# The experts' second bias: from a product ahead of each second layer to a loaded row that VectorE adds

## Chip, cores and metric

One core of one Trainium2 chip runs the whole kernel as one program. The metric is the device time of one execution in microseconds (us). Engine names as the profile has them: PE is TensorE, DVE is VectorE, ACT is ScalarE, POOL is GpSimd, SP is SyncE; L1279 is line 1279 of the kernel before.

## The reference, cut to what matters

A graph layer and a linear-attention layer are added onto 12,500 nodes of 256 values; then comes a layer of 8 experts of which each node uses one. The change is in the last lines: what an expert adds as `b2`.

```python
xn = layernorm(x)
x = x + gnn(xn, src, dst, edge_weight, ...) + mix(xn, ...)      # 212,500 edges
h = layernorm(x)
idx = argmax(softmax(h @ gate_w + gate_b))                      # 8 experts
prb = the probability of idx
pos = how many nodes before this one chose the same expert
kept = pos < C                                                  # C = ceil(1.25 * 12500 / 8) = 1954
buf[idx, pos] = h                                               # for the kept ones
hmid = relu(buf @ w1[e] + b1[e])                                # 256 -> 1024
ybuf = hmid @ w2[e] + b2[e]                                     # 1024 -> 256
y = ybuf[idx, min(pos, C - 1)] * (prb * kept)[:, None]
x = x + nan_to_num(y, posinf=10000, neginf=-10000)
```

## The kernel before, in words

The five engines run five programs that meet in semaphores; each engine's order is written out ahead of time. The order goes by *places*, 266 of them. At each of the first 208 (`PAIRS`) POOL gathers 8 chunks of 128 node rows for the edges (`gather_rows`, L967, one indirect DMA per chunk, two halves with the other POOL work of the place between them) and PE multiplies the place's 8 chunks into windows of sums (`multiply_pair`, L1079; the row buffers hold 6 places). What else is done at a place stands in the list `side`: "kv" (the attention's sums), "early" and "late" (the node tiles, `c_step`), "unit" (the experts), "end" (routing after place 208). A planner puts the experts' ticks there by estimated PE costs (`PE_PLACE`, `PE_EXPERT`, `PE_TURN`) and due times (`wanted_at`); the change leaves it as it is.

**Routing.** The node tiles are routed in 18 batches. When a batch's experts are chosen (`choose_expert`), its tokens ranked (`place_tokens`) and full tiles of 128 tokens of one expert found (`find_full`, `queue_units`), `fill_slots` writes for each tile which rows to gather (`gat_i`), where to scatter (`sca_i`), the probabilities (`sprb`) and the expert (`expert_i`), and raises `q_ready`. The last batch has what is left over: 22 tiles. In all there are 105 tiles (`SLOTS`) in K = 82 units: units 0 to 22 have two tiles, 23 to 81 one. Units 60 to 81 are the last batch.

**A unit's way.** POOL gathers its tokens' rows, 256 normalised values and 256 to add to (`gather_unit`, L987). PE transposes the first (L1238), ACT copies them (L2042). Then come ticks, 4 in a unit of two tiles and 2 in a unit of one: PE's first layer (L1261), ACT's relu with `b1` (L2059), and one tick later PE's second layer (`second_layer`, L1285), summed in one PSUM bank. After the last, ACT scales the sum by the probability into `tok` (L2065), and VectorE's `finish_unit` makes not-a-number to 0 and clips (L1816 to L1820), adds the row's old value (L1821) and raises `y_done`. Up to place 207 SP keeps the finished rows in DRAM (`keep_unit`, units 0 to 52, 76 tiles); POOL scatters them to the output after place 208, two or four tiles at a place, from a row buffer that SP reloads (`load_back`, L841, 8 tiles at a time, waiting for the scatters of the buffer's tiles before; `scatter_back`, L1008). Units 53 to 81 are scattered straight from `tok` (`scatter_unit`, L998).

**Weights.** 1 MB each for first and second layer, two buffers each. Up to unit 63 SP loads them: `load_first` (L815) when unit k-2's relu is done, `load_second` (L822) when its second layer is; each reads the expert's number first. SP's queue is in order. For units 64 to 81 (`SKIPS`) POOL issues them as indirect loads (`load_new_first` L1017, `load_new_second` L1025), where the rows of an expert that the buffer holds already are left out. In the last batch POOL has at each unit: L1017, L987, two L1008, L998, L1025.

**The second bias before.** At the laps step SP loads `ffn_b2` twice; `make_tables` splits it in a high and a low part (`b2_parts`, 16 rows: 2 x 8 experts); `fill_slots` makes for each tile a column with 1 in its expert's two rows (`expert_hot`, L1713). At a unit's first tick VectorE's `unit_tick` waits until PE has done the first tick of the previous unit's second layer and spreads that column over 128 columns (`hot_wide`, L1803, semaphore `hot_spread`). PE's `second_layer` begins, for each tile, with the product of `hot_wide` and `b2_parts` (L1279, 16x128 by 16x256 in f32r), onto which the layer's 8 products of 128x128 by 128x256 are summed.

## Time and profile before

| | |
|---|---|
| median of 3 runs | 2501.23 us (2500.39 to 2503.88) |
| the profiled execution | 2497.35 us, of which span 2495.6 us |
| granted TensorE clock, mean | 0.93 |
| busy: PE, DVE, ACT, POOL | 82%, 61%, 41%, 74% |
| DMA | 568.84 MB, mean 228 GB/s |
| SP's loads by size | weights 64 + 64 of 1,028 and 1,024 KB; most others 128 KB |

A row of the profile's groups reads: line, engine, operation, what it writes <- what it reads, shape, count | busy us in total, mean ns of one | idle us of the engine just before them, with what ended that idle time. A row of the timeline reads: start us, duration us, engine, line, operation [idle before <- releaser]. SPq is SP's DMA queue. A row by windows reads: stretch, its length, then busy us (and instructions) of PE, PE's weight loads, DVE, ACT, POOL, then the granted clock, the share of DMA busy, and GB/s. PE runs each f32 product as two instructions. A wait for several semaphores is put down to the one that came last by the profile, and "issue" is time in which an engine waited for nothing that the profile shows.

### The profile page before, as it was taken

Reading aid. Unit: us, or ns where it says so; the run is one execution under the profiler, and the core shown is the slowest. Engines: PE = TensorE matmul, PEld = TensorE weight load, DVE = VectorE, ACT = ScalarE, POOL = GpSimd, SP = SyncE. Lnnn points to the kernel's source line nnn. Section 1 sums busy time; section 2 is a strip of 40 time slices with the busy share of each in tenths; the row PEclk is TensorE's granted clock in tenths of the full one; section 3 lists DMA queues with packets and bytes.
Section 4 is the critical chain, followed back from the end, with each engine's and each line's share of the span. In section 5 each row is a group of like instructions: output and inputs, shape, how many; then the busy total and the mean of one; then the engine's idle time right before and its main releaser. Section 6 shows DMA issues by size and latency. Waiting matters only on the chain. (4 is left out here: it accounts for less than half of the span.)

```text
span 2495.6 us, 42607 instructions
## 1 busy us (share of the span) xinstructions
PE 2049.6 (82%) x12873; PEld 1578.1 (63%) x12873; DVE 1511.6 (61%) x5293; ACT 1033.6 (41%) x2479; POOL 1849.9 (74%) x1924
## 2 busy tenths in 40 slices
PE   0048999994677787998989989998989998787997
PEld 0015666662455565776768777776778777676986
DVE  6776555554358777787747556566565666565332
ACT  4663333331244444543434433443444444352332
POOL 7777777777777777777777777777777777765575
PEclk9999999996788887999999999999998999898999
DMA  9846666664566667777777777777887888778653
GB/s 337 321 138 178 174 175 175 175 172 128 150 195 201 194 190 255 237 238 222 244 232 227 248 231 234 233 229 253 304 295 273 306 304 293 249 274 305 239 180 108
DMA packets 279195, 568.84 MB, mean 228 GB/s; under 512 B 51493, under 2 KB 180142, under 8 KB 259791
## 3 DMA queue, kind: packets, MB, share of 16 engines
q0 software_dynamic: 98352, 268.90, 35.3%
q1 hardware_dynamic: 150225, 245.97, 28.9%
q10 hardware_dynamic: 30390, 51.21, 5.6%
q8 instruction: 108, 1.77, 0.3%
q14 instruction: 120, 0.98, 0.1%
HBM read 506.09 MB, written 87.86 MB: 238 GB/s over the span
## 5 line engine op out<-in xcount | busy, mean ns | idle before, releaser
L967 POOL DMA_INDIRECT rows_sb<-xn_scratch,src_sb x1517 | 1458.3, 961 | 462.2 <-issue 456.7
L1261 PE MATMUL bank<-acc 128*128 128x128 f32 (+1 forms) x2624 | 434.4, 319 | 3.6 <-ACT acc L2042 2.9
L1285 PE MATMUL bank<-acc 128*128 128x256 f32 x1680 | 413.1, 390 | 0.0
L1261 PEld LDWEIGHTS bank<-acc 128*128 128x128 f32 x2624 | 379.2, 202 | 27.3 <-issue 5.6
L1079 PE MATMUL bank<-rows_sb,s_sb 128*24 128x256 f32 x3082 | 229.7, 419 | 198.6 <-DMA rows_sb<-xn_scratch,src_sb 198.0
L2059 ACT ACTIVATE acc<-bank,acc 128x128 f32<-128x128 f32 (+1 forms) x656 | 211.9, 398 | 368.5 <-PE bank L1261 368.2
L1285 PEld LDWEIGHTS bank<-acc 128*128 128x128 f32 x1680 | 313.9, 194 | 48.8 <-issue 0.4
L1549 DVE TENSOR_TENSOR acc<-acc,bank 128x48 f32 x831 | 170.5, 205 | 264.8 <-PE bank L1089 150.2
L1079 PEld LDWEIGHTS bank<-rows_sb,s_sb 128*24 128x24 f32 x3082 | 85.5, 108 | 272.8 <-issue 240.4
L1976 ACT COPY sums<-bank 120x256 f32<-120x256 f32 x208 | 76.5, 368 | 355.6 <-PE bank L1079 355.5
L2007 ACT ACT_TABLE_LOAD x95 | 121.9, 1283 | 200.8 <-PE bank L1168 199.9
L1109 PE MATMUL bank<-arena 128*128 128x512 f32 x392 | 184.1, 592 | 0.0
L1153 PE MATMUL bank<-arena,weff 128*128 128x128 f32 (+1 forms) x784 | 124.3, 310 | 35.4 <-ACT arena L2031 35.4
L1153 PEld LDWEIGHTS bank<-arena,weff 128*128 128x128 f32 x784 | 114.9, 218 | 51.1 <-issue 48.3
L1625 DVE TENSOR_TENSOR arena<-bank,bias_sb 128x256 f32<-128x256 f32 x98 | 41.3, 422 | 171.9 <-PE bank L1168 171.7
L987 POOL DMA_INDIRECT acc<-h_scratch,gat_i x105 | 101.5, 966 | 37.5 <-issue 31.1
L1816 DVE TENSOR_TENSOR acc<-acc 128x256 int32<-128x256 f32 x105 | 45.0, 428 | 132.2 <-ACT acc L2065 126.5
L1164 PE MATMUL bank<-w2m_sb,arena 128*128 128x256 f32 x392 | 118.6, 432 | 2.6 <-DVE arena L1630 2.6
L1991 ACT ACTIVATE arena<-bank 128x512 f32<-128x512 f32 x98 | 58.5, 597 | 143.0 <-PE bank L1100 141.7
L1166 PE MATMUL bank<-w1g_sb,arena 128*128 128x256 f32 x392 | 112.5, 414 | 0.0
L1089 PE MATMUL bank<-ident,sums 120*128 120x120 f32 x416 | 81.3, 278 | 33.6 <-DVE acc L1549 33.4
L1563 DVE TENSOR_TENSOR arena<-bank,ss 128x512 f32<-128x512 f32 x98 | 67.8, 691 | 64.0 <-PE bank L1100 61.4
(277 smaller groups left out, 3633.7 us busy)
## 6 DMA issues: line engine op xcount, KB each, us to landing
acc<-ffn_first_in SPq DMA_DIRECT2D x64, 1028.0 KB
acc<-ffn_w_in SPq DMA_DIRECT2D x64, 1024.0 KB
arena<-xn_scratch SPq DMA_DIRECT2D x194, 128.0 KB, 3.1
h_scratch<-arena ACTq DMA_DIRECT2D x97, 256.0 KB
rows_sb<-xn_scratch,src_sb POOLq DMA_INDIRECT x1517
xnt_scratch<-arena SPq DMA_DIRECT2D x97, 128.0 KB, 2.3
arena<-xnt_scratch SPq DMA_DIRECT2D x97, 128.0 KB
arena<-x_in SPq DMA_DIRECT2D x97, 128.0 KB
```

What stands on the lines that cost most here:

```text
L967: pool.indirect_dma_start(out=chunk_row(c), out_offset=None, in_=xn_d, in_offset=bass.IndirectOffsetOnAxis(ap=src_sb[:, c:c + 1], axis=0)) ...
L987: pool.indirect_dma_start(out=tok[:, col % TOKENS, :], out_offset=None, in_=h2_d[0:tokens, :], in_offset=bass.IndirectOffsetOnAxis(ap=gat_ ...
L1079: m = pe.matmul(psum[0][i * COLS:i * COLS + WIN, 0:D], s_sb[:, p % S_SLOTS, i * GROUP + j, :], chunk_row(c), start=j == 0, stop=j == GROUP ...
L1109: m = pe.matmul(kv[0:r, :], xnt[:, t % R1, h, 0:r], wkv_sb[:, h, :], start=False, stop=h == H - 1)
L1153: m = pe.matmul(psum[2][:, f * P:f * P + r], weff[:, h, f * P:(f + 1) * P], c_xnt[:, t % XS, h, 0:r], start=h == 0, stop=h == H - 1)
L1164: pe.matmul(mix, c_hid[:, par, f, 0:r], w2m_sb[:, f, :], start=f == 0, stop=f == H - 1)
L1166: pe.matmul(gnn, c_xnt[:, t % XS, h, 0:r], w1g_sb[:, h, :], start=h == 0, stop=False)
L1261: m = pe.matmul(bank[:, i * tokens:(i + 1) * tokens], w1_sb[k % 2][:, h, f * P:(f + 1) * P], xt[:, k % 2, h, 0:tokens], start=h == 0, stop ...
L1285: m = pe.matmul(bank[:, i * D:(i + 1) * D], hid[:, f, i * P:(i + 1) * P], w2_sb[k % 2][:, f, :], start=False, stop=f == FC - 1 and i == 0)
L1549: dve.tensor_tensor(win, win, turned[:, :, i * COLS:i * COLS + WIN], ALU.add).then_inc(grp_added, 1)
L2007: act.activation(c_hid[:, par, f, 0:r], psum[2][:, f * P:f * P + r], ACT.Gelu, bias=beff[:, f:f + 1]).then_inc(c_gelu, 1)
L2059: act.activation(hid[:, f, 0:tokens], bank[:, i * tokens:(i + 1) * tokens], ACT.Relu, bias=b1_sb[k % 2][:, f:f + 1]).then_inc(l1_relu, 1)
```

## The change

The bias product, its split table, the one-hot columns and the copy that spread them are taken out. Instead there are two buffers of 128x256, `b2_sb`. SP loads for each unit the row `ffn_b2[expert]` into all 128 partitions (`load_bias`), at the place after the one where unit k-2 is finished, behind all else that SP has at that place, and waits for `y_done` of unit k-2. `finish_unit` waits for that load and begins for each tile with one operation more: y = bias x probability + y, ahead of the clean-up. The second layer's first product now starts the sum. The counts that `w2_ld` is waited for change as the two early loads go.

```diff
@@ -277,14 +277,12 @@
         w1_sb = [v[:, 0:H * FF].rearrange("p (h f) -> p h f", h=H) for v in first_sb]
         b1_sb = [v[:, H * FF:] for v in first_sb]
         w2_sb = [behind(0, FC, D) for _ in range(2)]
-        b2_parts, hot_wide = bkv_hl[0:2 * NE, 0:D], ones_r[0:2 * NE, :]
-        expert_hot = behind(1, SLOTS)[0:2 * NE, :]
+        b2_sb = [behind(1, D) for _ in range(2)]
         tok = behind(1, TOKENS, 2 * D)
         xt = behind(1, 2, H, UNIT)
         hid = behind(1, FC, UNIT)
         mask_sb = behind(1, D)
         clip_sb = behind(1, D)
-        b2_raw, b2_high = clip_sb[0:2 * NE, :], mask_sb[0:2 * NE, :]
 
         tab = behind(1, 2 * P)
         e_wide = behind(0, P)
@@ -294,8 +292,8 @@
         sel = behind(1, 2 * MOST_SLOTS)
         load_row = behind(1, MOST_SLOTS).bitcast(I32)
         sprb = behind(0, SLOTS)
-        (col_i, col_odd, col_tile, col_from, full_at, one_at, some_at, count, full, fresh, ranked, queue_at, queue_base, expert_no) = (
-            behind(0, 1) for _ in range(14))
+        (col_i, col_odd, col_tile, col_from, full_at, one_at, some_at, count, full, fresh, ranked, queue_at, queue_base) = (
+            behind(0, 1) for _ in range(13))
 
 
         ld_gmin, ld_edges, gmin_all = sem("ld_gmin"), sem("ld_edges"), sem("gmin_all")
@@ -307,7 +305,7 @@
             sem("early_stats"), sem("early_root"), sem("early_scaled"), sem("early_normed"))
         xn_ld, xnt_st = sems("xn_ld", R1), sems("xnt_st", R1)
         c_ld, cr_ld, c_st = sems("c_ld", XS), sems("cr_ld", RS), sems("c_st", OS)
-        w1_ld, w2_ld = sems("w1_ld", 2), sems("w2_ld", 2)
+        w1_ld, w2_ld, b2_ld = sems("w1_ld", 2), sems("w2_ld", 2), sems("b2_ld", 2)
         xs_ld, y_st = sems("xs_ld", 4), sems("y_st", YS)
         assert BACK_SLOTS * BACK_ROWS <= ROW_SLOTS
         kept_st, back_ld, back_st = sems("kept_st", YS), sems("back_ld", BACK_SLOTS), sems("back_st", BACK_SLOTS)
@@ -338,7 +336,7 @@
         q_fresh, q_selected, q_ready = sem("q_fresh"), sem("q_selected"), sem("q_ready")
         x_turned, x_copied = sem("x_turned"), sem("x_copied")
         l1_mm, l1_relu, l2_mm = sem("l1_mm"), sem("l1_relu"), sem("l2_mm")
-        y_scaled, y_done, hot_spread = sem("y_scaled"), sem("y_done"), sem("hot_spread")
+        y_scaled, y_done = sem("y_scaled"), sem("y_done")
 
 
         def halves(w):
@@ -607,11 +605,12 @@
             return e_place[last_tick[k] + FLUSH]
 
 
-        w1_at, w2_at, gather_at, scatter_at = ([[] for _ in range(PLACES)] for _ in range(4))
+        w1_at, w2_at, b2_at, gather_at, scatter_at = ([[] for _ in range(PLACES)] for _ in range(5))
         for k in range(K):
             known = slots_at[batch_of[k]] + 1
             w1_at[max([known] + [place_of(k - 1, 1)] * (k > 1))].append(k)
             w2_at[max([known] + [place_of(k - 1, 2)] * (k > 1))].append(k)
+            b2_at[max([known] + [done_place(k - 2) + 1] * (k > 1))].append(k)
             lag = wanted_at[k] - slots_at[batch_of[k]] - 1
             ahead = 1 if turn_place[k] < PAIRS + 2 else 3
             asked = max(known - 1 + lag, turn_place[k] - ahead)
@@ -652,7 +651,7 @@
             return 16 * ((k - SKIPS[0]) // 2 + 1)
 
         def w2_value(k):
-            return 16 * (k // 2 + 1) + 32 * (k % 2 == 0)
+            return 16 * (k // 2 + 1)
 
         def kv_steps(k, order):
             return [(k - s, s) for s in order if 0 <= k - s < T]
@@ -821,6 +820,13 @@
                     sp.wait_ge(l2_mm, l1_done(k - 2))
                 sp.dma_start(flat2(w2_sb[k % 2]), ffn_w2[bass.ds(x_, 1)].rearrange("a p f -> p (a f)")
                              ).then_inc(w2_ld[k % 2], 16)
+
+            def load_bias(k):
+                x_ = expert_of(k)
+                if k >= 2:
+                    sp.wait_ge(y_done, k - 1)
+                sp.dma_start(b2_sb[k % 2], ffn_b2[bass.ds(x_, 1), :].broadcast_to([P, D])
+                             ).then_inc(b2_ld[k % 2], 16)
 
             def keep_unit(k):
                 col, n = columns_of(k)[0], size(k)
@@ -859,8 +865,6 @@
                         for to, frm in ((w2m_sb[:, :, :], halves(mix_w2)), (w1g_sb[:, :, :], halves(gnn_w1t)),
                                         (w2g_sb[:, :, :], halves(gnn_w2t))):
                             sp.dma_start(to, frm).then_inc(wld2, 16)
-                        for part in range(2):
-                            sp.dma_start(b2_raw[part * NE:(part + 1) * NE, :], ffn_b2).then_inc(w2_ld[0], 16)
                     elif kind == "early":
                         for t, s in c_steps(k, (2, 0, 3)):
                             if s == 0:
@@ -879,6 +883,8 @@
                         load_second(k)
                 for k in keep_at[p]:
                     keep_unit(k)
+                for k in b2_at[p]:
+                    load_bias(k)
             for t in range(max(0, T - OS), T):
                 sp.wait_ge(c_st[t % OS], 32 * (t // OS + 1))
 
@@ -1272,18 +1278,13 @@
                         pe.wait_ge(new2_ld[k % 2], new_value(k))
                     else:
                         pe.wait_ge(w2_ld[k % 2], w2_value(k))
-                    pe.wait_ge(hot_spread, k + 1)
                     if y_bank_before(k) is not None:
                         pe.wait_ge(y_scaled, columns_of(y_bank_before(k))[-1] + 1)
-                    for i, col in enumerate(columns_of(k)):
-                        pe.matmul(bank[:, i * D:(i + 1) * D], hot_wide.bitcast(F32R), b2_parts.bitcast(F32R),
-                                  start=i == 0, stop=False)
-
                 for f in range(per_tick(k) * (j - 1), per_tick(k) * j):
                     tiles = range(size(k))
                     for i in tiles if f < FC - 1 else reversed(tiles):
                         m = pe.matmul(bank[:, i * D:(i + 1) * D], hid[:, f, i * P:(i + 1) * P], w2_sb[k % 2][:, f, :],
-                                      start=False, stop=f == FC - 1 and i == 0)
+                                      start=f == 0 and i == 0, stop=f == FC - 1 and i == 0)
                 m.then_inc(l2_mm, 1)
 
             def side_step(kind, k):
@@ -1668,14 +1669,6 @@
                 link(dve.tensor_scalar(some_at, col_tile, float(P), 1.0, ALU.mult, ALU.add))
                 for v in (tab, full, queue_at, queue_base):
                     link(dve.memset(v, 0.0))
-                link(dve.tensor_single_scalar(expert_no, ids[:, 0:1], 1.0, ALU.subtract))
-                link(dve.tensor_copy(whole, expert_no))
-                link(dve.tensor_single_scalar(whole, whole, NE - 1, ALU.bitwise_and))
-                link(dve.tensor_copy(expert_no, whole))
-                dve.wait_ge(w2_ld[0], 32)
-                link(dve.tensor_copy(b2_high.bitcast(F32R), b2_raw))
-                link(dve.tensor_tensor(b2_parts.bitcast(F32R), b2_raw, b2_high, ALU.subtract))
-                link(dve.tensor_copy(b2_parts[0:NE, :].bitcast(F32R), b2_high[0:NE, :]))
 
 
             def find_full(b):
@@ -1710,8 +1703,6 @@
                 token, chance, expert = (psum[6][:, SLOT_AT + i * n:SLOT_AT + (i + 1) * n] for i in range(3))
                 idf, empty = sel[:, 0:n], sel[:, MOST_SLOTS:MOST_SLOTS + n]
                 link(dve.tensor_copy(expert_i[:, here], expert[0:1, :]))
-                link(dve.tensor_scalar(expert_hot[:, here], expert[0:2 * NE, :], expert_no[0:2 * NE, :], None,
-                                       ALU.is_equal))
                 link(dve.tensor_scalar(gat_i[:, here], token, 1.0, 0.0, ALU.subtract, ALU.max))
                 link(dve.tensor_copy(sprb[:, here], chance))
                 link(dve.tensor_single_scalar(idf, token, 1.0, ALU.subtract))
@@ -1790,18 +1781,8 @@
                         if build_at[t] == k:
                             build_table(t)
                 elif kind == "unit":
-                    unit_tick(k)
                     if e_place[k] < PAIRS:
                         finish_unit(k)
-
-            def unit_tick(n):
-                k, j = e_ticks[n]
-                if k < K and j == 1:
-                    col = columns_of(k)[0]
-                    if k:
-                        dve.wait_ge(l2_mm, l1_value(k - 1, 1))
-                    dve.tensor_copy(hot_wide.bitcast(F32R), expert_hot[:, col:col + 1].broadcast_to([2 * NE, P])
-                                    ).then_inc(hot_spread, 1)
 
             def finish_unit(n):
                 for k in range(K):
@@ -1812,7 +1793,10 @@
                     dve.wait_ge(y_scaled, columns_of(k)[-1] + 1)
                     if k:
                         dve.wait_ge(y_done, k)
-                    for i in range(size(k)):
+                    dve.wait_ge(b2_ld[k % 2], 16 * (k // 2 + 1))
+                    for i, col in enumerate(columns_of(k)):
+                        link(dve.scalar_tensor_tensor(y[:, i, :], b2_sb[k % 2], sprb[:, col:col + 1], y[:, i, :],
+                                                      ALU.mult, ALU.add))
                         link(dve.tensor_tensor(mask, y[:, i, :], y[:, i, :], ALU.not_equal))
                         link(dve.copy_predicated(y[:, i, :], mask, nil[:, :].broadcast_to([P, D])))
                         link(dve.tensor_scalar(clip, y[:, i, :], 10000.0, -10000.0, ALU.min, ALU.max))
```

## Rows read from the trace of the kernel before

**Rows 1.** The page: busy time of the engines, and the costliest group

```profile
PE 2049.6 (82%) x12873; PEld 1578.1 (63%) x12873; DVE 1511.6 (61%) x5293; ACT 1033.6 (41%) x2479; POOL 1849.9 (74%) x1924
...
L967 POOL DMA_INDIRECT rows_sb<-xn_scratch,src_sb x1517 | 1458.3, 961 | 462.2 <-issue 456.7
```

**Rows 2.** Three stretches by engine (the view by windows)

```profile
1100.00:1300.00 200.00, 180.13 (x1108) 143.93 (x1106) 137.80 (x496) 86.79 (x194) 152.17 (x158) 0.97 0.75 243
2214.00:2302.00 88.00, 69.55 (x387) 59.31 (x384) 52.06 (x194) 28.24 (x82) 48.07 (x49) 0.86 0.79 293
2331.00:2473.00 142.00, 139.78 (x917) 126.31 (x917) 49.24 (x126) 54.39 (x180) 109.65 (x107) 1.00 0.53 180
```

**Rows 3.** One line, POOL's gathers of rows: shortest, median and longest in ns

```profile
L967 POOL DMA_INDIRECT rows_sb<-xn_scratch,src_sb x1517: 942/946/1382, 190.6 to 2208.8; - x190
```

**Rows 4.** Groups by line, of what goes and of what is like the addition

```profile
L1639 DVE SCALAR_TENSOR_TENSOR arena<-arena,c_sum 128x256 f32<-128x256 f32 x98 | 47.8, 487 | 3.4
...
L1279 PE MATMUL bank<-bkv_hl,ones_r 16*128 16x256 f32 x105 | 34.1, 360 | 11.4 <-ACT acc L2059 8.4 <-issue 2.9
...
L1803 DVE CAST ones_r<-acc 16x128 fp32r<-16x128 f32 x82 | 19.9, 243 | 39.1 <-PE bank L1285 34.8 <-DVE sca_i L1720 1.2
...
L1713 DVE TENSOR_SCALAR acc<-bank,acc 16x4 f32<-16x4 f32 (+4 forms) x16 | 3.4, 212 | 0.6
```

**Rows 5.** Timeline of POOL ahead of the last batch: start us, us, instruction

```profile
2235.07 1.05 POOL L998 DMA_INDIRECT out_dram<-acc,sca_i  x1 [2.89 <-DVE acc L1821]
```

**Rows 6.** Timeline of SP's queue in the same stretch

```profile
2253.86 0.33 SPq L841 DMA_DIRECT2D rows_sb<-kept_scratch  x1
2255.29 0.34 SPq L822 DMA_DIRECT2D acc<-ffn_w_in  x1
```

**Rows 7.** Timeline of PE, from there to the last batch

```profile
2266.35 0.35 PE L1279 MATMUL bank<-bkv_hl,ones_r 16*128 16x256 f32 x1 [1.83 <-ACT acc L2059]
...
2301.70 0.66 PE L1238 MATMUL bank<-ident,acc 128*128 128x128 f32 x2 [5.08 <-DMA acc<-h_scratch,gat_i]
...
2305.31 0.38 PE L1279 MATMUL bank<-bkv_hl,ones_r 16*128 16x256 f32 x1
```

**Rows 8.** Timeline of VectorE: the sums of the last batch are read

```profile
2274.88 0.22 DVE L1860 TENSOR_TENSOR arena<-bank,arena 128x56 f32<-128x56 f32 x1 [4.47 <-PE bank L1203]
```

**Rows 9.** Timeline of PE in the last batch

```profile
2328.56 0.38 PE L1279 MATMUL bank<-bkv_hl,ones_r 16*128 16x256 f32 x1
...
2336.32 0.38 PE L1279 MATMUL bank<-bkv_hl,ones_r 16*128 16x256 f32 x1
2336.63 2.00 PE L1285 MATMUL bank<-acc 128*128 128x256 f32 x8
...
2471.01 0.35 PE L1279 MATMUL bank<-bkv_hl,ones_r 16*128 16x256 f32 x1 [0.53 <-ACT acc L2059]
```

**Rows 10.** Timeline of POOL in the last batch

```profile
2330.73 1.05 POOL L1017 DMA_INDIRECT acc<-ffn_first_in,acc  x1 [6.90 <-ACT acc L2059]
...
2337.38 1.05 POOL L1025 DMA_INDIRECT acc<-ffn_w_in,acc  x1 [0.30 <-issue]
...
2445.09 1.23 POOL L1008 DMA_INDIRECT out_dram<-rows_sb,sca_i  x1 [0.30 <-issue]
...
2465.22 1.05 POOL L1025 DMA_INDIRECT acc<-ffn_w_in,acc  x1 [0.30 <-issue]
...
2471.93 1.05 POOL L1025 DMA_INDIRECT acc<-ffn_w_in,acc  x1 [0.30 <-DVE acc L1821]
```

**Rows 11.** Timeline of VectorE at 2445 us

```profile
2444.99 0.43 DVE L1816 TENSOR_TENSOR acc<-acc 128x256 int32<-128x256 f32 x1 [3.81 <-ACT acc L2065]
```

**Rows 12.** DMA issues: median us to landing of the second weights gathered by POOL

```profile
acc<-ffn_w_in,acc POOLq DMA_INDIRECT x18, 5.6
```

**Rows 13.** Timeline of all engines, the end

```profile
2482.58 0.47 ACT L2065 ACTIVATE acc<-bank,acc 128x256 f32<-128x256 f32 x1 [2.82 <-PE bank L1285]
...
2486.51 0.98 POOL L998 DMA_INDIRECT out_dram<-acc,sca_i  x1 [4.74 <-DVE acc L1821]
```

## The prediction

> **What bounds the kernel now.** I read the page first. By busy share PE looks like the bound (82%), but POOL's largest group, 1,517 gathers of rows, has 457 us of idle time that is put down to "issue": POOL waited for nothing, that is its own pace [rows 1]. The view by windows gives three stages. Up to the last gather of rows (2208.8) POOL has some 158 instructions in each 200 us, one per 1.26 us, busy 152 us; PE is busy for 180 and so has slack [rows 2, 3]. From 2214 to 2302 no engine is full, and the kernel follows a chain of waits that prepares the last batch of units. From 2331 to 2473 PE is busy for 139.8 of 142 us, which again looks like PE, but POOL has 107 instructions in it, busy 109.7 us, and with 0.30 us of issue before each that is 141.8 us: full as well [rows 2]. What the change is worth must be read stage by stage.
>
> **What goes and what comes.** For each of 105 tiles a product (L1279) of 0.36 us by the group, and for each of 82 units a copy on VectorE (L1803, 0.24 us), which also stood in a wait for PE; one compare per batch (L1713, 0.21 us) goes too. For each tile comes a scalar_tensor_tensor of 128x256 with a pointer scalar on two SBUF tensors. L1639 is that very form: 0.487 us, and 3.4 us of gaps over 98 of them, so 0.52 us each [rows 4]. For each unit SP issues one more load of 128 x 1 KB = 128 KB, 82 in all, 10.5 MB, beside 569 MB on the page.
>
> **Stage one, POOL's pace.** 53 of the 82 units, with 76 of the 105 tiles, are finished here. The products taken from PE are worth nothing, since PE has slack; the 76 additions (40 us) lie in VectorE's idle time (138 of 200 us busy [rows 2]); both are hidden by POOL's pace, and without that cover they would be 76 x 0.3 us less and up to 40 us more. The new load stands in SP's queue behind keep_unit of the same unit k-2, which waits for the same count of y_done, so nothing behind it (the loads of the node tiles, the next weights) waits longer than now. Eight small operations and two loads at the start of this stage go, hidden too. What can change is POOL's pace itself. The gathers take 0.946 us at the median and 0.961 in the mean, up to 1.38 [rows 1, 3]: 1,517 x 0.015 = 23 us in excess, and over VectorE's 1,512 us of work [rows 1] that is 0.015 us per us. 40 us more, some 15 fewer: +0.4; I take +0.5, ends 0 and 76 x 0.25 = +19 (0.25 is the largest excess seen in the last stage, below).
>
> **Stage two, the chain to the last batch.** I followed it backwards. POOL's scatter of unit 53 starts at 2235.07 after 2.89 us of waiting for VectorE's last add of that unit [rows 5]. Behind it on POOL stand the scatters that free a row buffer; SP's reload of that buffer (L841) waits for them, and SP's load of unit 57's second weights (L822, 2255.29) stands right behind that reload, at 2253.86 [rows 6]. PE waits for those weights at 2266.35 (1.83 us; the view names ACT, but I take the weights, whose load needed these 11 us in a crowded stage) [rows 7], after that come the sums of the last batch, and VectorE is released by them at 2274.88 [rows 8]; from there it works without a break to the queue of units, and PE starts the last batch's first transposition at 2301.70, behind the gather of its tokens [rows 7]. On this chain lie: the addition for unit 53, +0.52; one 128 KB load ahead of unit 57's weights, 128 KB at the 293 GB/s of this stage [rows 2], +0.45; the product of unit 57, which comes after the wait, -0.3; the compare before q_ready, -0.21 [rows 4]. Sum +0.5. No row shows how a row of 1 KB read 128 times lands: the lower end is 0, the upper that of a load of 1 MB, 5.6 us [rows 12]; I take the bytes, as other loads in this queue are 128 KB as well. SP itself needs for a load with its expert's number at most the 1.43 us from L841 to L822 [rows 6], 82 x 1.43 = 117 us of a queue that mostly waits; here it lies ahead of the reload, inside SP's wait for POOL. Other waits could also shrink, so ends -1.5 and +5.
>
> **Stage three, the last 22 units.** PE's unit takes 2336.32 - 2328.56 = 7.76 us when nothing holds it, the product in it 2336.63 - 2336.32 = 0.31 [rows 9]. POOL's cycle has six instructions: from its load of second weights at 2337.38 to that at 2471.93 are 17 cycles, 7.91 us each, with 0.30 us of issue as the only idle time [rows 10]. So POOL is the slower of the two by 0.15 us a unit, and PE shows it: it gains on POOL through units whose weights needn't be fetched, and stops where they must. The load issued at 2465.22 lands 5.6 us later by the median [rows 12], at 2470.8; PE's product of that unit starts at 2471.01 after a wait [rows 9]. With 0.31 us less per unit PE only reaches each such stop sooner and waits longer. What counts:
> - POOL's full stretch begins at 2330.73, when ACT has finished unit 62 [rows 10]. The products of units 59, 60 and 61 (the first at 2305.31 [rows 7]) come between 2301.70 and that: -0.93.
> - The stretch itself: no instruction goes or comes. One of its scatters, with VectorE's two-input L1816 running as it began (2444.99), took 1.23 us where the last scatter of all takes 0.98 (in the chain of the end, below) [rows 10, 11]. One more such operation per unit: +0.3, ends 0 and 22 x 0.25 = +5.5.
> - The 128 KB loads beside the weights' loads: most fall between two of them, +0.2, ends 0 and 22 x 0.7 (128 KB at 180 GB/s [rows 2]), of which only the 6 or so that PE waits for count, +4.
> - Behind the last stop the products of units 80 and 81 go: -0.6.
> - The end: from ACT's scaling at 2482.58 to the last scatter at 2486.51 is one chain on VectorE [rows 13], with one addition more: +0.52.
>
> **Sum:** +0.5 +0.5 -0.93 +0.3 +0.2 -0.6 +0.52 = +0.5 us. The profiled execution took 2497.35 us (span 2495.6 and 1.75 around it) and would take 2497.8; the median of the three runs is 3.9 us above it and even their lowest 3.0 above, so I carry the same step over: 2501.23 + 0.5 = **2501.7 us**. About 0.2%, 5 us, is what a measurement of this kernel can tell from no change.
>
> **A rule that speaks against the change.** POOL's longest scatter of the last stage began with a two-input operation of VectorE at work [rows 10, 11]; yet the gathers' mean is only 0.015 us over their median [rows 1, 3], with VectorE busy for 69% of the time beside them [rows 2]. The Trainium skill, GPSIMD Engine Reference, section 1 (Specifications), says that GpSimd shares its SBUF interfaces with VectorE, with contention from instructions in a 2-port mode or with two SBUF inputs. By that rule, the trace agrees in kind, and the addition is of the kind that contends; taken at full strength it gives the second rival below rather than the +0.8 in my sum.
>
> **The rivals.**
> - *PE is the bound of the last stage.* For it: 139.8 of 142 us busy. Then all 23 products from unit 59 to 81 count, 23 x 0.31 = 7.1, less 0.52 at the end: 6.6 us faster, 2494.6. Against it: PE's stops at loads that POOL issued, and POOL's 7.91 against 7.76. Chance 0.10.
> - *The additions slow POOL* (slower). Place: VectorE's additions meet POOL's gathers in stage one, and its scatters and loads in stage three, both at POOL's pace. Price: each of the 105 additions that costs POOL 0.1 us gives 10.5 us, 2511; it decides from 0.05 us each. For it: the 1.23 us scatter and the mean above the median. Against: 1,512 us of VectorE's work cost 23 us now. Chance 0.08.
> - *The bias row's load delays stage two* (slower). SP has the loads in one queue, DMA is 0.79 busy there [rows 2], and if a broadcast row took the time of a 1 MB load the second weights of unit 57, and with them the last batch, would be 5 us later: 2506.5. Chance 0.07.
> - *The change doesn't take the product away*: excluded by the diff; but the wait of VectorE for PE at L1803 goes as well (34.8 us [rows 4]). If that wait held up the chain of stage two, 1 to 3 us would be won: 2500. Inside "same".
>
> **How the numbers follow.** My forecast, no difference, has 0.73; the rest is spread over the rivals, with 0.02 for a faster stage two. Faster by over 0.2%: 0.12; within: 0.73; slower: 0.15. The range: the sum's small ends (-1.5 in stage two, none of the delays) together with part of the first rival reach down to 2496.5; the bounds of stage two and of the last stage taken together, halfway, reach up to 2506.5. The spread of the runs shown (2500.4 to 2503.9) lies within. About 0.1 is left out on each side.
>
> **What would show it.** Right: L1279, L1803 and L1713 gone, 105 additions of 0.49 us, 82 loads of 128 KB; the last gather of rows still at 2209 give or take 1; POOL's cycle in the last batch still 7.9 us, PE's free unit 7.45 and its waits ahead of the second layer longer, 0.53 growing to about 1.1 at unit 80; last-batch start near 2302; one addition more on the final chain. Wrong: a POOL cycle under 7.8, which would say that PE set it; a cycle or a gather longer by 0.05 us or more; or a last batch that starts after 2305, behind weights that landed late.

## The result and the profile after

The change made the kernel slower: 2510.10 us (2504.52 to 2517.59, 8 runs) against 2500.63 us (2496.06 to 2503.88, 8 runs) of the kernel before in the same comparison, ratio 1.0044, 95% interval [1.0030, 1.0059]. A later comparison gave 1.0063 [1.0049, 1.0077]. The forecast was no difference, at most 2506.5 us. The traced execution took 2513.21 us (span 2511.5), 3 us above its median, and that of before lay 4 us below the median given for it: the 15.9 us between the two spans are more than the change costs.

The page of the kernel after, with the groups of POOL's gathers and of the addition; they answer to [rows 1, 3, 4]:

```profile
PE 2025.0 (81%) x12768; PEld 1572.8 (63%) x12768; DVE 1543.5 (61%) x5293; ACT 1033.2 (41%) x2479; POOL 1850.4 (74%) x1924
...
DMA packets 290974, 579.58 MB, mean 231 GB/s; under 512 B 52790, under 2 KB 191919, under 8 KB 271568
...
L973 POOL DMA_INDIRECT rows_sb<-xn_scratch,src_sb x1517 | 1458.7, 962 | 464.0 <-issue 457.0
...
L1798 DVE SCALAR_TENSOR_TENSOR acc<-acc 128x256 f32<-128x256 f32 x105 | 50.9, 484 | 167.8 <-ACT acc L2049 161.0
```

The parts are as foreseen: PE has 105 instructions and 24.6 us of work less, the addition takes 0.484 us, 10.7 MB more are moved. By windows, as in [rows 2]:

```profile
1100.00:1300.00 200.00, 183.40 (x1120) 148.24 (x1118) 143.79 (x510) 90.00 (x203) 152.43 (x157) 0.96 0.78 251
2214.00:2302.00 88.00, 70.19 (x387) 60.90 (x388) 51.99 (x190) 30.33 (x83) 45.34 (x46) 0.85 0.78 288
2331.00:2473.00 142.00, 128.94 (x854) 118.53 (x853) 49.55 (x119) 51.92 (x174) 99.55 (x97) 0.98 0.58 196
```

In the last stage PE is idle for 13 us of 142 where it was for 2, and POOL gets 97 instructions done, not 107. Both are short of full now: they stop for each other. The start of the last batch is later too (timelines of PE and VectorE, kernel after; they answer to [rows 7, 8]):

```profile
2275.49 3.41 PE L1286 MATMUL bank<-acc 128*128 128x256 f32 x8 [4.34 <-issue]
...
2283.09 0.22 DVE L1844 TENSOR_TENSOR arena<-bank,arena 128x56 f32<-128x56 f32 x1 [6.11 <-PE bank L1209]
...
2308.85 0.41 PE L1244 MATMUL bank<-ident,acc 128*128 128x128 f32 x2 [4.17 <-DMA acc<-h_scratch,gat_i]
```

It starts at 2308.85, not 2301.70; that is 7.2 us, of which 3.6 us were there at the last gather of rows (2212.35, not 2208.80). The prediction had named the chain rightly (PE stops at 2275.49 ahead of the second layer of unit 57, whose second weights are issued 10.2 us before; the same sums release VectorE), but gave it 0.5 us. POOL's timeline answers to [rows 10, 13]:

```profile
2336.52 1.05 POOL L1023 DMA_INDIRECT acc<-ffn_first_in,acc  x1 [5.76 <-DMA out_dram<-acc,sca_i]
...
2343.08 1.08 POOL L1031 DMA_INDIRECT acc<-ffn_w_in,acc  x1 [0.30 <-issue]
...
2486.04 1.12 POOL L1031 DMA_INDIRECT acc<-ffn_w_in,acc  x1 [1.33 <-PE bank L1286]
...
2502.38 0.99 POOL L1004 DMA_INDIRECT out_dram<-acc,sca_i  x1 [4.23 <-DVE acc L1805]
```

The 17 cycles of POOL from 2343.08 to 2486.04 take 8.41 us each, not 7.91. Two of PE's stops in them, 3.46 and 3.33 us, where PE had none over 0.8 in this trace of before (a second trace of it has one of 1.54):

```profile
2346.36 2.15 PE L1286 MATMUL bank<-acc 128*128 128x256 f32 x5 [3.46 <-issue]
...
2382.32 1.91 PE L1267 MATMUL bank<-acc 128*128 128x128 f32 x15 [3.33 <-issue]
```

### The profile page after: what moved, and what is told of

Read it like the earlier page. It is cut to its first block and busy times, and to the rows that moved or that the text cites. A ratio compares the mean times of both kernels' runs of the same rounds, so it can differ in the third digit from the quotient of the medians.

```text
span 2511.5 us, 42810 instructions
## 1 busy us (share of the span) xinstructions
PE 2025.0 (81%) x12768; PEld 1572.8 (63%) x12768; DVE 1543.5 (61%) x5293; ACT 1033.2 (41%) x2479; POOL 1850.4 (74%) x1924
## 5 line engine op out<-in xcount | busy, mean ns | idle before, releaser
L1267 PE MATMUL bank<-acc 128*128 128x128 f32 (+1 forms) x2624 | 441.5, 322 | 13.8 <-issue 8.8
L1267 PEld LDWEIGHTS bank<-acc 128*128 128x128 f32 x2624 | 385.8, 205 | 38.0 <-issue 14.3
L1286 PEld LDWEIGHTS bank<-acc 128*128 128x128 f32 x1680 | 319.7, 196 | 65.2 <-issue 12.5
L1798 DVE SCALAR_TENSOR_TENSOR acc<-acc 128x256 f32<-128x256 f32 x105 | 50.9, 484 | 167.8 <-ACT acc L2049 161.0
```

Source lines behind the costliest of these rows:

```text
L1267: m = pe.matmul(bank[:, i * tokens:(i + 1) * tokens], w1_sb[k % 2][:, h, f * P:(f + 1) * P], xt[:, k % 2, h, 0:tokens], start=h == 0, stop ...
L1286: m = pe.matmul(bank[:, i * D:(i + 1) * D], hid[:, f, i * P:(i + 1) * P], w2_sb[k % 2][:, f, :], start=f == 0 and i == 0, stop=f == FC - 1 ...
```

## The experiments

The letters: `a_` and `after_` are versions of the change, `b_` is the kernel before with loads added, `c_` the kernel before with work of VectorE added, `d_` the kernel before with the product taken away, `e_` the change with another source for its loads. Ratios are to the kernel before in the same comparison; its median moved between 2498.1 and 2503.2 us from one comparison to the next, so ratios and not times are compared.

| kernel | median us | ratio | 95% interval |
|---|---|---|---|
| the change | 2510.10 | 1.0044 | 1.0030 to 1.0059 |
| `after_again`, the same | 2512.92 | 1.0063 | 1.0049 to 1.0077 |
| `before_again`, control | 2496.76 | 1.0001 | 0.9991 to 1.0011 |
| `d_noprod`, product away | 2500.15 | 1.0002 | 0.9992 to 1.0012 |
| `c_adds`, 105 additions | 2504.70 | 1.0027 | 1.0017 to 1.0036 |
| `c_kept`, 76 of them (units 0 to 52) | 2507.38 | 1.0024 | 1.0013 to 1.0034 |
| `c_last`, 29 of them (53 to 81) | 2504.31 | 1.0007 | 0.9998 to 1.0016 |
| `c_twice`, 210 additions | 2508.64 | 1.0045 | 1.0032 to 1.0058 |
| `c_single`, one-input operations | 2506.00 | 1.0013 | 1.0003 to 1.0022 |
| `b_loads`, 82 loads | 2508.96 | 1.0039 | 1.0027 to 1.0051 |
| `b_free`, 82 loads, no wait for `y_done` | 2511.35 | 1.0031 | 1.0020 to 1.0043 |
| `b_last`, 22 loads (60 to 81) | 2507.21 | 1.0014 | 1.0004 to 1.0024 |
| `b_skip2`, 80 loads | 2506.13 | 1.0024 | 1.0011 to 1.0037 |
| `b_thin`, 82 loads of 4 KB | 2502.05 | 1.0016 | 1.0007 to 1.0025 |
| `b_thin_free`, the same, no wait for `y_done` | 2504.03 | 1.0007 | 0.9998 to 1.0016 |
| `a_noload`, the change without its loads | 2505.03 | 1.0022 | 1.0012 to 1.0032 |
| `e_distinct`, 128 different rows | 2511.99 | 1.0039 | 1.0025 to 1.0053 |
| `after_later` | 2513.23 | 1.0043 | 1.0030 to 1.0057 |
| `after_moved` | 2511.08 | 1.0040 | 1.0027 to 1.0053 |

### The three parts by themselves

Three theories stood after the first trace, and the texts below call them by number: 1, the 82 loads get in the way of other loads and of the chains; 2, PE with less work reaches its stops sooner, stands longer, and gets a lower clock; 3, the additions on VectorE slow POOL or delay the chains.

The product taken away (and the copy that spread its column):

```diff
-                    pe.wait_ge(hot_spread, k + 1)
-                    for i, col in enumerate(columns_of(k)):
-                        pe.matmul(bank[:, i * D:(i + 1) * D], hot_wide.bitcast(F32R), b2_parts.bitcast(F32R),
-                                  start=i == 0, stop=False)
...
-                    unit_tick(k)
```

> The kernel before without the product L1279, the copy L1803 and its wait; the second bias is left out. Theory 2: slower, ratio 1.001 to 1.004. Theories 1 and 3: 0 to 2 us faster, ratio 0.9985 to 1.000; were PE the bound of the last stage, 0.997.

Measured: 1.0002. The row by windows of the last stage:

```profile
2331.00:2473.00 142.00, 133.30 (x895) 122.54 (x894) 43.73 (x107) 54.39 (x180) 106.71 (x104) 0.99 0.54 184
```

PE is idle for 8.7 us of it, not 2.2 [rows 2], and POOL's last load of second weights starts 170.0 us after the first transposition, as before (170.2). Inside these 170 us something was won and lost again: the first load of second weights starts 34.1 us after the first transposition, where before has 35.7, and the 17 cycles of POOL from there take 8.00 us each, where before has 7.91. POOL's cycle holds this stage; a faster PE only waits more.

The additions (of zeros, onto the kernel before), and the loads (read by nobody, into edge weights that are used up by then; this first version also waited for the load before to land):

```diff
+                    for i, col in enumerate(columns_of(k)):
+                        link(dve.scalar_tensor_tensor(y[:, i, :], bkv_hl[:, D:2 * D], sprb[:, col:col + 1], y[:, i, :],
+                                                      ALU.mult, ALU.add))
```

> The kernel before with one more scalar_tensor_tensor per tile in finish_unit, which adds zeros. Theory 3: ratio 1.003 to 1.005. Theories 1 and 2: between 0.999 and 1.001 (0.5 us at the end, 0.5 us ahead of the last batch).

```diff
+                sp.wait_ge(y_done, k - 1)
+                sp.wait_ge(b2_ld, 16 * k)
+                sp.dma_start(wgt_sb[:, 0:D], ffn_b2[bass.ds(x_, 1), :].broadcast_to([P, D])).then_inc(b2_ld, 16)
```

> The kernel before with the 82 loads of the bias row added at the same places and with the same wait, into a part of the weights of edges that is no longer read; nobody uses them. Theory 1: slower by the whole loss or more, ratio 1.003 to 1.006. Theories 2 and 3: no difference, 0.999 to 1.001.

The change with loads for units 0 and 1 alone (`if k >= 2: return` in `load_bias`):

> The changed kernel with the row loaded for units 0 and 1 alone; the addition stays for every tile, so the other units add a wrong expert's bias. Theory 1 (the 82 loads get in the way of the weights' loads and of the chains that free row buffers): nearly all of the 0.4% goes, ratio to the kernel before 0.998 to 1.001. Theory 2 (PE with less work reaches its stops sooner, stands longer, and its clock falls): the loss stays, ratio 1.003 to 1.005. Theory 3 (the additions on VectorE slow POOL or delay the chains): the loss stays as well, 1.003 to 1.005.

Additions 1.0027 (6 to 7 us), loads 1.0039 (about 10 us), product nothing, the change without its loads 1.0022. 0.27% and 0.31 to 0.39% make 0.6 to 0.7%; the change has 0.44 and 0.63%, and its three variants further below have 0.39 to 0.43%, so together the parts may cost somewhat less than their sum. Both added parts are real costs: neither interval reaches 1.

### Controls

> The kernel before, unchanged, as a control of the measurement and for a second trace: ratio 1.000 within 0.001. In the kernels that do the same as before up to unit 53 the last gather of rows came 5 us later than in the first trace of before; if that trace was an early one by chance, this one has its last gather at 2212 to 2215; if not, at 2209.

> The change, unchanged, for a second trace and a closer ratio: 1.0044 again. From its last gather of rows to the first transposition of the last batch 96 to 98 us (kernels without the loads there took 93 to 97.6), and from that to POOL's last load of second weights over 173 us (170.0 to 170.6 without loads, 170.8 to 177.2 with them).

The control came out at 1.0001, with its last gather at 2206.98: the first trace of before was no early one. The kernels whose last gather came at 2214 or 2215 without an addition in stage one (`c_last`, `b_last`, `b_free`) stood in the comparison in which before had its slowest median, 2503.23. So single landmarks are compared within a kernel only, as distances. Three of them, worked out from the timelines of one trace each: A, from the start of POOL's last gather of rows to PE's last pair; B, from the same gather to the first transposition of the last batch, so that A is a part of B; C, from that transposition to POOL's last load of second weights. D is the sum, over the gathers of rows that overlap an operation of `finish_unit`, of their time above 0.946 us. One trace says little: two traces of the same kernel differ by up to 1.4 us in A and B and 2.8 us in C (before and after).

| | A us | B us | C us | D us |
|---|---|---|---|---|
| before, `before_again` | 5.1, 5.7 | 92.9, 92.1 | 170.2, 170.3 | 9.0, 7.5 |
| `d_noprod` | 9.4 | 97.6 | 170.0 | 8.6 |
| `c_adds`, `c_kept` | 3.9, 5.0 | 94.1, 91.9 | 170.0, 171.8 | 14.2, 13.0 |
| `c_last`, `c_twice` | 5.0, 5.1 | 95.5, 95.6 | 172.7, 173.0 | 7.6, 13.5 |
| `c_single` | 5.2 | 94.5 | 172.4 | 11.8 |
| `b_loads`, `b_free` | 11.0, 10.9 | 100.0, 99.0 | 173.8, 173.5 | 9.1, 10.3 |
| `b_last`, `b_skip2` | 5.8, 5.2 | 95.9, 93.0 | 175.6, 172.9 | 9.0, 8.0 |
| `b_thin`, `b_thin_free` | 5.8, 7.0 | 90.6, 93.4 | 178.6, 173.4 | 8.5, 8.6 |
| `a_noload` | 7.1 | 93.3 | 170.6 | 13.1 |
| after, `after_again` | 8.8, 10.2 | 96.5, 97.9 | 177.2, 174.4 | 10.6, 13.1 |
| `e_distinct`, `after_later` | 8.1, 9.4 | 96.0, 96.2 | 170.8, 173.5 | 12.7, 12.7 |
| `after_moved` | 8.6 | 96.1 | 173.4 | 13.2 |

### Where additions cost

> The kernel before with the addition (of zeros) for units 53 to 81 alone, 29 of 105. If additions cost by slowing POOL's gathers in stage one (gathers that an addition overlaps took 0.045 us more, 76 x 0.045 = 3.4 us), this gives ratio 1.0005 or less; if they cost on the chain of stage two and in the last batch (one late VectorE operation per unit, then POOL's scatter), about the whole 0.27%: ratio 1.002 to 1.003.

> The kernel before with the addition (of zeros) for units 0 to 52 alone, 76 of 105, all beside POOL's gathers of rows. All 105 gave 1.0027, the last 29 gave 1.0007 (0.9998 to 1.0016). If stage one is where additions cost, 1.0020 and a last gather of rows about 6 us later than a kernel without additions in the same comparison; if not, under 1.0010.

> The kernel before with two additions of zeros for each tile in place of none (one gave 1.0027). If each addition has its price (it slows the POOL instruction that it overlaps, and lengthens what VectorE does before a scatter), two give twice that: 1.0045 to 1.0055, and gathers that an addition overlaps are about 0.04 us longer. If the first one only tipped something over, or the 1.0027 was chance, two give 1.002 to 1.003.

The three edits of `c_adds`: `if k >= 53:`, `if k < 53:` and `for _ in range(2):` ahead of the addition. The 76 additions of stage one gave 1.0024, nearly all of the 1.0027; the last 29 gave 1.0007, an interval that reaches no change. Twice as many gave 1.0045. POOL's gathers, group row of `before_again` and then of `c_kept`:

```profile
L967 POOL DMA_INDIRECT rows_sb<-xn_scratch,src_sb x1517 | 1457.0, 960 | 462.2 <-issue 457.3
```

```profile
L967 POOL DMA_INDIRECT rows_sb<-xn_scratch,src_sb x1517 | 1464.6, 965 | 464.2 <-issue 456.8
```

The same 1,517 instructions took 7.6 us more here; over all traces column D is cleaner. It is 7.5 to 10.3 us in ten traces without additions in stage one, mean 8.6, and 10.6 to 14.2 in eight traces with one for each tile, mean 12.8; the gathers that overlap nothing of `finish_unit` keep 13.4 to 18.3 us in all, with the same mean in both groups (15.7 and 15.3). So with the additions the gathers beside `finish_unit` take 4.2 us more, 0.056 us for each of the 76. The last gather comes 5.1 us later on average (2215.3, not 2210.1); the rest is about what POOL itself waits more, for PE above all, beyond its usual 0.31 us: 2.1 us in these eight traces, 0.6 in the ten.

Two things speak against reading 0.056 us as the price of an addition. With twice as many (`c_twice`) D is 13.5, no more than with one, and the last gather came at 2214.2; only its B and C (95.6 and 173.0) are above those of `c_adds`, so what the second addition costs isn't explained by the gathers. And in `after` the gathers that overlap an addition itself took 0.017 us above 0.946, in five other traces 0.038 to 0.048; those beside the three operations right behind it in `after` took 0.060 to 0.067 (0.015 to 0.030 beside the same operations in before). That additions cost in stage one is shown; how, only in part.

Two inputs or one: for each tile two operations `y = y x 1 + 0` that read one tile only, in place of the addition.

```diff
+                        for _ in range(2):
+                            link(dve.tensor_scalar(y[:, i, :], y[:, i, :], 1.0, 0.0, ALU.mult, ALU.add))
```

> The kernel before with, for each tile, two operations of VectorE that read one tile only (y = y x 1 + 0, 128x256, some 0.25 us each) in place of one addition that reads two in SBUF (0.48 us): the same time on VectorE. If what slows POOL is VectorE's instructions with two inputs in SBUF, this costs nothing: under 1.0005, and the gathers they overlap take the median. If it is VectorE being busy in SBUF, or its time before y_done, as much as an addition: 1.002 to 1.003.

```profile
L1817 DVE TENSOR_SCALAR acc<-acc 128x256 f32<-128x256 f32 x210 | 69.9, 333 | 127.9 <-ACT acc L2067 118.7 <-DVE arena L1746 1.9 <-DVE sca_i L1720 1.0
```

They keep VectorE for 0.67 us a tile, more than the addition's 0.49, and cost 1.0013, half as much, with D at 11.8. The intervals of 1.0013 and 1.0024 overlap, so this ranks the two only weakly; that one-input operations are free is unlikely, since the interval (from 1.0003) leaves out no change, and D lies above all ten values without additions. The Trainium skill, GPSIMD Engine Reference, section 1 (Specifications), puts the contention down to instructions with two SBUF inputs or in a 2-port mode; no run here shows which mode these operations used, so that one-input operations contend too doesn't speak against it.

### Where loads cost: DMA time or SP's queue

`b_free`: the loads go to two places in turn, and SP waits for no `y_done`, only for the landing of the load before last.

```diff
-                sp.wait_ge(y_done, k - 1)
```

> The kernel before with the 82 loads of the bias row added (into columns of a table that is used up by then, read by nobody), without any wait for y_done: SP issues each where it comes in its order. Two theories of what the loads cost. Traffic: the 10.5 MB (or the 128 descriptors of 1 KB each) take time from gathers and weights, then this costs the same as the loads with a wait did, ratio 1.003 to 1.004. Queue: SP stands in a wait for y_done of unit k-2 and what is behind it (weights of units up to 63, reloads of row buffers) is late, then this costs under 0.1%, ratio 1.0000 to 1.0010, and the first transposition of the last batch is back within 2 us of where it is without loads.

`e_distinct`, in the change:

```diff
-                sp.dma_start(b2_sb[k % 2], ffn_b2[bass.ds(x_, 1), :].broadcast_to([P, D])
+                sp.dma_start(b2_sb[k % 2], ffn_w2[bass.ds(x_, 1), :, 0:D].rearrange("a p f -> (a p) f")
```

> The change, but each of the 82 loads reads 128 different rows of 1 KB (a column block of the second weights) in place of one row 128 times; the values added are wrong for it. If reading one address 128 times is what makes the load dear, this is near the version without loads: ratio to before about 1.002 and SP-issued second weights land as without loads. If it is the bytes, the 128 descriptors or the place in SP's queue, it stays at the change's 1.0044.

`b_thin` and, without the wait, `b_thin_free`:

```diff
-                sp.dma_start(wgt_sb[:, (k % 2) * D:(k % 2 + 1) * D], ffn_b2[bass.ds(x_, 1), :].broadcast_to([P, D])
+                sp.dma_start(wgt_sb[:, (k % 2) * D:(k % 2) * D + 8], ffn_b2[bass.ds(x_, 1), 0:8].broadcast_to([P, 8])
```

> The kernel before with 82 loads added, each in the place and with the wait for y_done that the change has, but of 128 pieces of 32 bytes in place of 1 KB (4 KB a load instead of 128 KB), read by nobody. If the loads cost by their bytes in the DMA engines, nearly nothing is left: ratio 1.000 to 1.001. If they cost by their count of pieces, or by SP's time and place in its queue, it stays at 1.003 to 1.004.

> As the loads of 32-byte pieces, but without the wait for y_done: SP issues each where it comes. With the wait these cost 1.0016, and in that trace the reload at the start of the last batch was issued 2 us later than before (25.0 against 22.9 us after the first transposition), after which weights fetched by POOL landed late and PE and POOL stopped for each other. If the wait in SP's order is what the thin loads cost, this is within 0.05% of before and the reload is back at 23 us; if it is the 128 pieces themselves, it stays at about 1.0016.

The page's queue of SP (packets, MB, share of 16 engines' span), in this order for before, `b_free`, `e_distinct` and `b_thin`:

```profile
q1 hardware_dynamic: 150225, 245.97, 28.9%
```

```profile
q1 hardware_dynamic: 162033, 256.72, 30.8%
```

```profile
q1 hardware_dynamic: 162001, 256.71, 30.3%
```

```profile
q1 hardware_dynamic: 162033, 246.31, 29.2%
```

Times the spans (2495.6, 2511.7, 2506.0 and 2501.5 us) that is 721, 774, 759 and 730 us of all 16 engines: 0.64 us for a load of the broadcast row, 0.46 for one of 128 different rows, 0.11 for one of 4 KB. These are differences of whole queues, so what the other loads of SP took more is in them. The forecast had 0.45. Without SP's wait the loads still give 1.0031. With different rows the change is at 1.0039 where it was at 1.0044 and 1.0063: the repeated address is not the main cause; its interval (1.0025 to 1.0053) leaves room for a small share. With 4 KB and no wait 1.0007 is left, an interval that reaches no change. That points to the bytes, for the whole kernel. For the last batch it doesn't: there the two kernels with 4 KB loads have C at 178.6 and 173.4 us, no less than those with 128 KB loads. The Trainium skill, DMA: Bandwidth & Descriptors, Rules for kernel authors, says that under 64 KB a transfer is mostly overhead. The shares agree: by the 0.46 us of 128 KB the bytes of 4 KB would take 0.014 us, and such a load took 0.11. Yet in the kernel's time this overhead hardly shows.

With the wait the 4 KB loads cost 1.0016. The intervals of the two overlap, but the trace shows a way. SP's timeline at the start of the last batch, `before_again` and then `b_thin`:

```profile
2319.72 0.33 SPq L815 DMA_DIRECT2D acc<-ffn_first_in  x1
2322.02 0.33 SPq L841 DMA_DIRECT2D rows_sb<-kept_scratch  x1
```

```profile
2320.71 0.34 SPq L818 DMA_DIRECT2D acc<-ffn_first_in  x1
2321.88 0.33 SPq L836 DMA_DIRECT2D wgt_sb<-ffn_b_in  x1
2323.86 0.33 SPq L855 DMA_DIRECT2D rows_sb<-kept_scratch  x1
```

The new load, which waits for VectorE, now stands ahead of the reload: 3.15 us from the first weights to the reload, where it was 2.30 (2.64 in the first trace of before). The reload is issued 25.0 us after the first transposition, where it was 22.9; 1.2 us of that lateness were there at the first weights already. The reload's 1 MB then comes nearer to the weights that POOL fetches; PE and POOL of `b_thin`:

```profile
2344.39 0.35 PE L1298 MATMUL bank<-bkv_hl,ones_r 16*128 16x256 f32 x1 [1.57 <-ACT acc L2078]
2344.67 3.35 PE L1304 MATMUL bank<-acc 128*128 128x256 f32 x8
```

```profile
2352.68 1.06 POOL L1044 DMA_INDIRECT acc<-ffn_w_in,acc  x1 [1.50 <-PE bank L1304]
2355.94 1.01 POOL L1036 DMA_INDIRECT acc<-ffn_first_in,acc  x1 [2.19 <-ACT acc L2078]
```

PE waits 1.57 us for second weights, then its eight products take 3.35 us, not the 2.00 of [rows 9]; the granted clock is 0.66 from 2344 to 2349 and 1.00 before and after. A unit later POOL waits 1.50 and 2.19 us for PE and ACT, 3.1 us beyond its usual 0.30 each. So a stop of 1.6 us can grow: both engines are nearly full, each waits for the other, and the clock adds to it. That the reload made these weights late is argued from one trace. A test in the change itself, with the bias rows of units 60 to 81 one place later, behind that reload:

```diff
-            b2_at[max([known] + [done_place(k - 2) + 1] * (k > 1))].append(k)
+            b2_at[max([known] + [done_place(k - 2) + 1 + (k >= 60)] * (k > 1))].append(k)
```

> The change with the bias row of units 60 to 81 loaded one place later, so that at place 225 it stands behind the reload of row buffers and the second weights of unit 63, not ahead of them. If SP's wait ahead of the reload is part of what the loads cost in the last batch, this is 0.05 to 0.15% faster than the change (1.0044 and 1.0063 in its two comparisons, so 1.004 to 1.005 here) and the reload is issued 23 to 24 us after the first transposition; if only the bytes count, no difference. Neither theory has it faster than before.

1.0043: between the two ratios of the change or at one of them, so this doesn't show a gain, and the reload came at 24.7 us, not clearly sooner than the change's 25.8 and 24.0. SP's wait as a cause is not shown.

### Which loads cost

`b_last` and `b_skip2` have the loads of `b_free` with the wait, for `k >= 60` and for `k not in (53, 54)`.

> The kernel before with the bias-row loads of units 60 to 81 alone (22 of 82, 2.8 MB), with the wait for y_done as in the change, read by nobody. If the loads cost in the last batch, where PE waits for weights that POOL fetched (landing a little late, POOL then waiting for PE), this gives most of the 0.39%: ratio about 1.003. If they cost before it (gathers of stage one, or the chain of stage two), ratio under 1.001 and POOL's cycle in the last batch stays at 7.9 to 8.0 us.

22 loads, all in the last batch, gave 1.0014; C was 175.6 us where kernels without loads there have 170.0 to 173.0 (nine traces, mean 171.2). All nine traces with 1 KB loads in the last batch have 170.8 to 177.2, mean 173.9: 2.7 us. The two with 4 KB loads have a mean of 176.0, so that these 2.7 us come from the bytes is not shown.

The rest is in column B, and there in A. PE's pairs at the end of stage one, in the kernel before and then after:

```profile
2203.08 1.06 PE L1079 MATMUL bank<-rows_sb,s_sb 128*24 128x256 f32 x16
2207.36 1.06 PE L1079 MATMUL bank<-rows_sb,s_sb 128*24 128x256 f32 x16 [0.34 <-DMA rows_sb<-xn_scratch,src_sb]
2213.87 1.05 PE L1079 MATMUL bank<-rows_sb,s_sb 128*24 128x256 f32 x10
```

```profile
2204.84 1.06 PE L1085 MATMUL bank<-rows_sb,s_sb 128*24 128x256 f32 x16 [1.06 <-DVE s_sb L1530]
2211.65 1.06 PE L1085 MATMUL bank<-rows_sb,s_sb 128*24 128x256 f32 x16 [3.08 <-DMA rows_sb<-xn_scratch,src_sb]
2221.16 1.05 PE L1085 MATMUL bank<-rows_sb,s_sb 128*24 128x256 f32 x10
```

PE stops 3.08 us for rows that land late, and then needs 9.51 us to the last pair where it needed 6.51. The windows of that stretch, before and after:

```profile
2207.50:2215.00 7.50, 6.95 (x58) 5.04 (x51) 5.89 (x24) 4.26 (x8) 3.78 (x4) 1.00 0.63 184
```

```profile
2214.00:2222.00 8.00, 7.65 (x32) 6.07 (x32) 3.11 (x13) 3.69 (x6) 1.48 (x2) 0.60 0.40 114
```

The granted clock is 0.60 instead of 1.00: most of the stretch, behind the stop, at 1.2 GHz in place of 2.4. What comes ahead of the late rows is in SP's timeline after, and what follows:

```profile
2192.62 0.33 SPq L828 DMA_DIRECT2D acc<-ffn_b_in  x1
...
2197.73 0.33 SPq L828 DMA_DIRECT2D acc<-ffn_b_in  x1
...
2222.32 0.81 SPq L847 DMA_DIRECT2D rows_sb<-kept_scratch  x2
...
2263.86 0.33 SPq L847 DMA_DIRECT2D rows_sb<-kept_scratch  x1
2265.31 0.33 SPq L821 DMA_DIRECT2D acc<-ffn_w_in  x1
```

Two bias rows, of units 53 and 54, are issued 20 and 15 us ahead of the last gather, in a stretch in which DMA is nearly full (2190 to 2210, before and after):

```profile
2190.00:2210.00 20.00, 18.52 (x144) 14.39 (x143) 16.55 (x64) 10.64 (x27) 15.18 (x16) 1.00 0.89 303
```

```profile
2190.00:2210.00 20.00, 17.51 (x130) 14.37 (x128) 17.32 (x68) 10.88 (x28) 15.12 (x17) 1.00 0.96 314
```

They aren't needed until places 209 and 211. The first reload of the row buffers waits for the last pair, so it starts 10.0 us after the last gather, not 6.2, and the whole chain of stage two hangs on it. The test leaves out just these two (of the 82, in the kernel before):

> The kernel before with 80 of the 82 bias-row loads, waits for y_done included, all but those of units 53 and 54, read by nobody. In every trace with loads of 1 KB pieces these two are issued 18 to 20 and 11 to 15 us ahead of the last gather of rows, and PE then waits 2.5 to 4.1 us for the last rows and does its last pair 8.1 to 11.0 us after the last gather (3.9 to 7.1 us in kernels with the product and without such loads). Theory: these two loads take DMA time from the last rows, and 3 to 4 of the 8 to 10 us that the loads cost are theirs: then ratio 1.002 to 1.0025 and the last pair 4 to 7 us after the last gather. Rival (the loads' cost is spread over all, 0.1 us each): ratio 1.003 to 1.004 and the last pair still 8 us or more behind.

```profile
2202.95 1.06 PE L1098 MATMUL bank<-rows_sb,s_sb 128*24 128x256 f32 x16
2207.36 1.06 PE L1098 MATMUL bank<-rows_sb,s_sb 128*24 128x256 f32 x16 [0.48 <-DMA rows_sb<-xn_scratch,src_sb]
2213.87 1.05 PE L1098 MATMUL bank<-rows_sb,s_sb 128*24 128x256 f32 x10
```

The wait and the slow clock are gone, A is 5.2 and B 93.0 us, and the ratio is 1.0024. This is one trace, of a run 4 us below the kernel's median (2502.03, 2506.13), and the ratio's interval overlaps that of all 82 loads. It fits the rest, though: of the thirteen traces with the product, the two with these loads of 1 KB pieces have A at 11.0 and 10.9 and a granted clock of 0.56 and 0.55 between the last two pairs, and the eleven without them, or with 4 KB ones, have 3.9 to 7.0, ten of them at 1.00 (`b_thin_free`, the eleventh, at 0.79). In the kernel with the product these two loads bring the slow clock. The change with these two moved behind the last pair:

```diff
-            b2_at[max([known] + [done_place(k - 2) + 1] * (k > 1))].append(k)
+            b2_at[209 if k in (53, 54) else max([known] + [done_place(k - 2) + 1] * (k > 1))].append(k)
```

> The change with the bias rows of units 53 and 54 loaded at place 209 (behind the first reloads and the second weights of unit 55) in place of 203 and 204. If those two loads hold up the last rows, the last pair comes 5 to 9 us after the last gather (8.8 to 10.2 with the change; 9.4 and 7.1 in the two kernels that had neither product nor load) and the ratio falls from 1.0044 and 1.0063 by about 0.001, to 1.0035 to 1.0045. If not, or if VectorE now waits for the bias of unit 53 ahead of POOL's scatter, no difference. Slower than before in either case.

Here A stayed at 8.6 and the ratio at 1.0040. PE's pair at the stop in `after_moved`, and the row by windows from there to its last pair:

```profile
2215.27 1.06 PE L1085 MATMUL bank<-rows_sb,s_sb 128*24 128x256 f32 x16 [1.68 <-DMA rows_sb<-xn_scratch,src_sb]
```

```profile
2215.27:2224.76 9.49, 8.93 (x46) 7.11 (x46) 3.56 (x18) 4.23 (x7) 3.40 (x4) 0.64 0.47 140
```

The kernels without the product show the other half. `d_noprod` has no load and no addition:

```profile
2206.80 1.92 PE L1079 MATMUL bank<-rows_sb,s_sb 128*24 128x256 f32 x16 [2.69 <-DMA rows_sb<-xn_scratch,src_sb]
```

```profile
2206.80:2217.80 11.00, 10.45 (x47) 7.74 (x47) 3.24 (x16) 4.23 (x7) 3.83 (x5) 0.54 0.40 122
```

With less work of its own PE waits 2.69 us there (1.41 in `a_noload`) and gets the lower clock as well. All seven traces without the product have a granted clock of 0.54 to 0.64 between the last two pairs and A at 7.1 to 10.2, with the two loads or without. So in the change either cause is enough, and taking the loads away doesn't help. What this costs the kernel is less sure than the landmark: `d_noprod` has A and B 4 to 5 us above before and a ratio of 1.0002.

## Why the prediction was wrong

The stages, the bound of each, and the chain of stage two were right. Three terms of the sum were too small, and each had its true size within the end that was written beside it; the range took these ends only in part. Two of the forecast's own signs of being wrong came in the first trace: a last batch that starts after 2305 (2308.85) and a cycle of POOL longer by 0.05 us or more (8.41).

- **Stage one, "40 us more, some 15 fewer: +0.4; I take +0.5".** The step that failed first: the excess of all gathers was spread over all of VectorE's work, 0.015 us per us. But gathers beside `finish_unit` already had 0.047 us each where others had 0.012 (column D of before: 9.0 us on 192 gathers, 15.4 on 1,325). Additions stand exactly there; with them these gathers take 4.2 us more and the last one comes 5.1 us later. The rival that decided "from 0.05 us each" is half of what happened (`c_adds`: 6 to 7 us for 105); it had a chance of 0.08.
- **Stage two, "one load of 128 KB ahead of unit 57's weights, +0.45".** The size of a load was nearly right (0.46 to 0.64 us of all 16 engines); the place where the stage is lengthened was wrong. It is ahead of the stage, at the last gathers of rows, where PE now stops for rows and goes on at the lower clock. Two other loads, 15 and 20 us before the last gather, do that in a kernel with the product; taking the product away, which the prediction put at nothing there because PE has slack, does it without any load. DMA was 0.89 busy there before. Column B is 93.9 us on average over the 13 traces in which these two loads are absent or of 4 KB (`after_moved` aside), and 97.6 over the six with them: +3.7 in place of +0.5. Column A grows by as much, 5.8 to 9.7. In the change itself the loads' share of this isn't shown: of the seven traces without the product the four with these loads have B at 96.6 on average, the three without at 95.7. The chain was followed back to a reload, but not to what that reload waits for (the last pair) and to what the last pair waits for (rows).
- **Stage three, "-0.93, -0.6" and "+0.2" for the loads.** The products of units 59 to 61, 80 and 81 were counted as gains, 1.5 us. The traces have them: without the product POOL's first load of second weights comes 34.1 to 34.3 us after the first transposition, with it 35.6 to 36.8, and in `d_noprod` the time behind the last such load is 22.9 us, not 23.7. But the 17 cycles between take 8.00 us in place of 7.91 and give 1.5 us back, and with the loss ahead of the batch `d_noprod` is at 1.0002. That interval (from 0.9992) can't exclude a gain of 1.5 us. And with the loads column C is 2.7 us longer, within the end of +4. "No instruction goes or comes" held for POOL; what changed is when its weights land.
- **"Nothing behind it waits longer than now"** held in stage one, where the load stands behind a wait for the same count. In the last batch the load of unit 62 stands ahead of a reload, and that reload came 25.8 and 24.0 us after the first transposition, where before has 23.2 and 22.9. Whether that costs is open (`after_later`).
- **What held:** the product is worth nothing in the kernel's time (the rival of 2494.6 fell); the addition's 0.48 us; POOL's cycle as the bound of the last stage, 7.9 to 8.1 us in kernels without loads.

Sum as measured: gathers 4.2, stage two 3.7, last batch 2.7, and an estimate of 1 for the final chain and the addition of unit 53, 11.6 us; the change measured 11 to 16 us (0.44 and 0.63%). The terms are means over traces of different kernels and good to 1 or 2 us each, so that they meet the lower measurement so closely is in part luck. What stays open: how the second addition of `c_twice` costs; how the loads' cost in the change divides over the three stages; whether SP's wait has a share of its own in it; and how much of an addition's cost is its second input.
